# A three-block perceiver on one core: the first rounds re-ordered, the last ones written out by themselves

## The chip, the cores and the metric

The kernel runs on one core of one Trainium2 chip. The metric is the device time of one execution in microseconds (us), and the figure that counts is the median over the runs.

## The reference, cut to what matters

The batch is 32 sequences of 64 rows (x) with a context of 128 rows each; every row has 512 features, all in 32-bit floats.

```python
def reference(x, ctx, ...):
    x = x + xattn(layernorm(x), ctx)   # 16 heads, latent size 32, softmax over 128 keys
    x = x + attn(layernorm(x))         # one head of 128, softmax over 64 keys, then Wo and bo
    x = x + ffn(layernorm(x))
    return x

def ffn(x):
    xh = x @ hadamard
    step = clip(max|xh| per row, 1e-5) / 7
    xq = clip(round(xh / step), -8, 7) * step
    scale = clip(mean|weight| per row of weight, 1e-5)
    wq = where(weight > scale/2, 1, where(weight < -scale/2, -1, 0)) * scale
    return xq @ wq.T
```

## The kernel before

Two sequences make a pair, which fills the 128 partitions; there are 16 pairs (`PAIRS`). Every engine runs the same software pipeline, written as `body(i, ...)` for a round i. A round works on four pairs at once: `front` is pair i+1 (projections of queries and context, and the raw scores of the 16 heads), `cross` is pair i (maxima, 256 exponentials of 128 columns over all pairs, so 16 a round; their transposes; the weighted sum u), `self_` is pair i-1 (the product with Wv, xo; the residual x2; its normalised form x2n; the second attention; x3) and `quant` is pair i-2 (the Hadamard product, the 4-bit quantiser, the product with the ternary weights, the result). Rounds go from -1 to 17. Rounds -1 to 3 and 12 to 17 are unrolled by `pipeline` and `looped`, rounds 4 to 11 run in a hardware loop of two rounds. Stages whose pair does not exist are left out, so that round 15 has no front, round 16 no front and no cross, round 17 only quant.

Nothing plans the order: each engine executes its own list in the order in which `body` writes it, and waits on semaphores: `made[...]` is raised by TensorE (PE) when a PSUM bank is filled, `read[...]` by the engine that has emptied it, `done[...]` by VectorE (DVE), ScalarE (ACT) or GpSimd (POOL). So a wait in one engine's list holds everything written behind it on that engine. PSUM has eight banks: 0 to 3 hold the scores of one pair and then their transposes, B1 to B4 are shared by the other stages in turn.

The parts that matter here, with the line numbers of the profile. On PE: `keep_busy` (L589) issues matmuls on constants that nobody reads; `wide_bias` (L604), `wide_scale` (L610), `hadamard_mean` (L617) and `ternary_transposed` (L627) prepare the weights; `transposed` (L638) turns the exponentials; L648 is xo, L655 turns x3, L691 the Hadamard product, L698 turns x2n, L706 and L709 are `projected`, L729 and L733 queries, keys and values of the second attention, L741 the query projection of two pairs at once in the odd rounds, L786 u, L806 the scores of the next pair, L829 the integer product (L824 its last one in halves), L838 the output projection. On ACT: the exponentials (L320), and all copies out of PSUM under the one line L314. On DVE: `largest` (L450 the maxima of 8 heads, L454 their scaled negatives nmx), `sums` (L459), `ternary` (L429 to L442), the quantiser (L499 to L511), x3 (L580). On POOL: `hadamard_centred` (L274), x2n (L284), x2b (L298), the result (L307).

The weights are prepared within the first rounds. In round 0 DVE runs `ternary` in one piece behind the maxima of pair 0: the sizes of all weight rows (L429), then eight passes that make the ternary matrix, then `const_row`; only behind them come the sums of pair 0 and the maxima of pair 1. PE runs `keep_busy(10, B3)` ahead of the first `transposed` and `keep_busy(4, B3)` behind the last; both `ternary_transposed` stand at the end of round 0. In round 1 PE computes `hadamard_mean` between the projections and the turning of x2n. In rounds 15 to 17 the order is that of every other round, with `keep_busy` in eight places, 29 of its matmuls in all (58 instructions of the trace).

## Time and profile before

| | |
|---|---|
| median of 3 runs | 324.0 us (323.95, 324.0 and 1033.37) |
| profiled execution, its own time | 324.15 us |
| span from first to last instruction in it | 322.4 us |
| busy share of the span | PE 96%, DVE 76%, ACT 65%, POOL 27% |
| granted TensorE clock, mean | 0.999 |

The span is what the trace shows; 1.75 us of the execution's own time lie around it. Busy time of PE counts the constant matmuls of `keep_busy` too. PE's matmuls are pipelined, so that one alone looks longer than its share of a run of them: twenty matmuls of 128 columns take 2.39 us, 0.11 us each. A matmul on 32-bit floats is two instructions in the trace, a transpose of them is one.

### The profile page before, as it was taken

The page shows a single profiled execution, that of the slowest core. Times are in us where ns is not written, and L with a number is a line of the kernel's source. Part 1 is how long each engine was busy: PE and PEld are TensorE (multiplying, and loading weights), DVE is VectorE, ACT ScalarE, POOL GpSimd, SP SyncE. Part 2 cuts the span into 40 slices and gives each one's busy share as a digit, 9 for nine tenths or more (in the row PEclk, how much of TensorE's full clock was granted, in tenths as well). Part 3 has the DMA queues.
Part 4 walks back from the last instruction along what each step waited for, and adds up shares of the span by engine and source line. Part 5 has one row for each costly group of instructions (what it writes and reads, how often), then busy time and mean ns, then how long its engine had stood idle before and what let it go on. Part 6 is the DMA issues. An engine that isn't in the chain of part 4 may idle for free.

```text
span 322.4 us, 8517 instructions
## 1 busy us (share of the span) xinstructions
PE 310.4 (96%) x3172; PEld 219.1 (68%) x3172; DVE 244.9 (76%) x524; ACT 209.5 (65%) x590; POOL 88.4 (27%) x129
## 2 busy tenths in 40 slices
PE   7987999999999999999999999999999999999995
PEld 6875776768576866667576867666675867675754
DVE  1499558887889878887889778987888877986435
ACT  1395867768596777767686777766776869582310
POOL 2000544041223324140323224240414123232320
PEclk9999999999999999999999999999999999999999
DMA  7891402050301403050302302050401010000000
GB/s 205 299 380 63 166 3 98 2 165 32 108 27 38 161 2 130 0 193 2 130 0 89 107 33 98 0 195 0 130 3 68 0 68 2 33 3 33 0 35 33
DMA packets 13481, 25.25 MB, mean 78 GB/s; under 512 B 3216, under 2 KB 3984, under 8 KB 13456
## 3 DMA queue, kind: packets, MB, share of 16 engines
q1 hardware_dynamic: 13456, 24.91, 22.4%
q8 instruction: 16, 0.26, 0.3%
q14 instruction: 9, 0.07, 0.1%
HBM read 20.71 MB, written 4.19 MB: 77 GB/s over the span
## 4 chain that ended last, share of the span: by engine, by line
PE 77%; DVE 10%; ACT 7%; issue 2%; DMA 1%; SPq 0%; POOL 0%; DVEq 0%
PE ps L691 12%; PE ps L729 8%; PE ps L638 7%; PE ps L806 6%; PE ps L786 5%; PE ps L648 4%; PE ps L829 4%; PE ps L838 4%; ACT prob L320 4%; PE ps L733 4%; DVE mx L450 3%; PE ps L709 2%; PE ps L741 2%; PE ps L669 2%; PE ps L812 2%
## 5 line engine op out<-in xcount | busy, mean ns | idle before, releaser
L320 ACT ACTIVATE prob<-ps,nmx,qk_scale 128x128 f32<-128x128 f32 x256 | 96.1, 468 | 40.5 <-DVE nmx L454 40.5
L691 PE MATMUL ps<-had_s,x3t 128*128 128x512 f32 x128 | 59.0, 604 | 1.1 <-ACT x3t L314 0.8
L450 DVE TENSOR_REDUCE mx<-ps 128x8 f32<-128x1024 f32 x32 | 38.9, 1216 | 11.1 <-PE ps L806 11.1
L691 PEld LDWEIGHTS ps<-had_s,x3t 128*128 128x128 f32 x128 | 23.0, 189 | 30.2 <-issue 28.4
L459 DVE TENSOR_REDUCE sum_a<-prob 128x8 f32<-128x1024 f32 x32 | 38.1, 1210 | 2.6 <-ACT prob L320 2.6
L303 POOL TENSOR_TENSOR qk_scale<-aux,power 128x1 f32<-128x1 f32 x16 | 8.8, 548 | 103.9 <-DVE aux L540 103.9
L314 ACT ACTIVATE prob_t<-ps 128x512 f32<-128x512 f32 x64 | 35.2, 622 | 0.6
L638 PE MATMUL ps<-ident,prob 128*128 128x128 f32 x256 | 33.7, 275 | 0.6 <-ACT prob L320 0.6
L729 PE MATMUL ps<-x2t,wqkv_s 128*128 128x128 f32 x256 | 32.7, 281 | 0.6 <-ACT x2t L314 0.2
L307 POOL TENSOR_TENSOR res<-prod,x 128x512 f32<-128x512 f32 x15 | 19.1, 1272 | 47.1 <-DVE prod L573 47.1
L729 PEld LDWEIGHTS ps<-x2t,wqkv_s 128*128 128x128 f32 x256 | 29.8, 191 | 2.6 <-ACT x2t L314 1.8
L638 PEld LDWEIGHTS ps<-ident,prob 128*128 128x128 f32 x256 | 28.5, 141 | 2.4 <-ACT prob L320 1.5
L648 PEld LDWEIGHTS ps<-wv_bd,u_t 128*128 128x128 f32 x128 | 16.7, 191 | 9.1 <-issue 9.1
L281 POOL TENSOR_TENSOR rstd<-aux,power 128x1 f32<-128x1 f32 x16 | 8.8, 548 | 44.6 <-DVE aux L479 44.6
L298 POOL TENSOR_TENSOR x2b<-x,const_row 128x512 f32<-128x512 f32 x16 | 20.3, 1271 | 0.1
L806 PE MATMUL ps<-ckv,q_t 32*64 32x128 f32 x1024 | 19.3, 278 | 0.1
L648 PE MATMUL ps<-wv_bd,u_t 128*128 128x128 f32 x128 | 16.9, 275 | 1.7 <-issue 1.7
L786 PE MATMUL ps<-prob_t,ckv_k 128*32 128x256 f32 x256 | 17.1, 385 | 0.7 <-ACT q_t L314 0.5
L589 PE MATMUL ps<-mean_w 128*128 128x128 f32 x102 | 15.9, 299 | 1.4 <-POOL p L261 1.4
L499 DVE TENSOR_REDUCE amax<-ps 128x1 f32<-128x512 f32 x16 | 11.0, 689 | 8.1 <-PE ps L691 7.9
L806 PEld LDWEIGHTS ps<-ckv,q_t 32*64 32x64 f32 x1024 | 15.5, 130 | 2.4 <-issue 0.7
L589 PEld LDWEIGHTS ps<-mean_w 128*128 128x128 f32 x102 | 14.3, 209 | 4.0 <-issue 2.2
(120 smaller groups left out, 552.7 us busy)
## 6 DMA issues: line engine op xcount, KB each, us to landing
ct<-ctx_cols SPq DMA_DIRECT2D x16, 512.0 KB, 4.6
xt<-x_cols SPq DMA_DIRECT2D x16, 256.0 KB, 2.7
xr<-x_rows SPq DMA_DIRECT2D x16, 256.0 KB, 4.3
y<-res SPq DMA_DIRECT2D x15, 256.0 KB, 2.0
w_rows<-weight SPq DMA_DIRECT2D x1, 1024.0 KB, 8.8
had_s<-hadamard SPq DMA_DIRECT2D x1, 1024.0 KB, 9.0
wqkv_s<-wqkv SPq DMA_DIRECT2D x1, 768.0 KB, 10.6
wqk<-w_qk SPq DMA_DIRECT2D x2, 128.0 KB, 4.5
```

The lines of the kernel that those rows point to most:

```text
L298: nc.gpsimd.tensor_tensor(x2b[:], x2[:], const_row[:], ALU.add).then_inc(done["x2b"], 1)
L314: return nc.scalar.activation(dst, src, ACT.Copy)
L320: last = nc.scalar.activation(prob[:, h, :], ps[:, h // 4, (h % 4) * P:(h % 4) * P + P], ACT.Exp, bias=nmx[:, h:h + 1], scale=qk_scale[:])
L450: V.tensor_reduce(mx[:, h], ps[:, 2 * half:2 * half + 2, :].rearrange("p r (c k) -> p (r c) k", c=EC), AX.X, ALU.max).then_inc(done["mx"], 1)
L459: V.tensor_reduce(sum_a[:, h], prob[:, h, :], AX.X, ALU.add).then_inc(done["sum"], 1)
L589: pe.matmul(ps[:, bank, 0:P], mean_w[:], mean_w[:], start=True, stop=True)
L638: mm = pe.transpose(ps[:, r, c * P:(c + 1) * P], prob[:, 4 * r + c, :], ident[:])
L648: mm = pe.matmul(ps[:, B1, c * P:(c + 1) * P], u_t[:, c, :], wv_bd[:, c, :], start=True, stop=True)
L691: mm = pe.matmul(ps[:, B4, :], x3t[:, c, :], had_s[:, c, :], start=(c == 0), stop=(c == EC - 1))
L729: mm = pe.matmul(ps[:, B1, s * P:(s + 1) * P], wqkv_s[:, c, s * P:(s + 1) * P], x2t[:, c, :], start=(c == 0), stop=(c == EC - 1))
L786: mm = pe.matmul(ps[32 * r:32 * r + 32, B2, :].rearrange("p (c t) -> p c t", c=EC) [:, :, 64 * bb:64 * bb + 64], ckv_k[:, bb, :], prob_t[: ...
L806: mm = pe.matmul(ps[64 * bb:64 * bb + 64, r, c * P:(c + 1) * P], q_t[g, 1 - par, bb, c, :], ckv[g, 1 - par, bb * SKV:(bb + 1) * SKV], star ...
```

## The change

Rounds are re-ordered at both ends; the arithmetic stays, and rounds 3 to 14 are as before. `N` is 15, the last pair. New buffers are added for the last pair's quantiser (`x3t_n`, `aux3_n`, `step_n`, `prod_n` and so on).

At the front. SP issues `had_s`, `w_rows` and the second `load_rows` earlier and `wqkv_s` behind the loads of pair 2. In round 0 PE runs `projected`, the Hadamard mean in two halves, all four `transposed`, `wide_bias` and then the scores of pair 1 ahead of u; DVE takes over three of ACT's copies (q_t, ckv and the first prob_t), and computes only the weight sizes and scales ahead of both maxima of pair 1. The ternary matrix is made in four pieces: three in round 1, the fourth in round 2 between the maximum of the Hadamard product (L499) and the step (L504); its transposes are two halves, one late in round 1, one in round 2 between the values and `transposed(2)`, with ACT's copy of 1024 columns ahead of its copies prob_t 2 and 3. On POOL `hadamard_centred` goes to the start of round 1, behind the first nmx of pair 1. In round 1 PE runs `transposed(2)`, `transposed(3)`, the turning of x2n and the query projection ahead of the second attention's queries.

At the back. From the end of round 14 each engine has a list of its own. The calls of PE and DVE are in the diff; ACT's and POOL's follow the same order of pairs, ACT with all sixteen exponentials of pair 15 together (only the copies of x3t between the sixth and seventh). The maxima of heads 8 to 15 of pair 15 are first in DVE's list; pair 15's xo follows its u directly; the quantiser of pair 14 runs beside the second attention of pair 15. In the text below the written-out part is called the tail. `keep_busy` is called there with 4, 2, 4, 14 and 4. The helpers (`attended`, `head`, `quantized` and so on) issue the same instructions as `body` did, with bank and pair as arguments, and are not shown.

```diff
-        def looped(eng, body):
+        N = PAIRS - 1
+
+        def looped(eng, body, end):
             at = pipeline(body)
             with eng.Fori(*LOOP) as j:
                 body(j * 2, j, 0, True, True, True, True)
                 body(j * 2 + 1, j, 1, True, True, True, True)
-            for i in range(2 * LOOP[1], PAIRS + 2):
+            for i in range(2 * LOOP[1], end):
                 at(i)
...
+            sp.dma_start(had_s[:], hadamard.rearrange("(c p) n -> p c n", p=P)).then_inc(ld_w["had"], 16)
+            sp.dma_start(w_rows[:], weight.rearrange("(c p) n -> p c n", p=P)).then_inc(ld_w["w"], 16)
+            load_rows(1, 1)
             for s in range(3):
                 sp.dma_start(b_qkv[:, s:s + 1], bqkv.rearrange("(s p o) -> s p o", p=P, o=1)[s]).then_inc(ld_w["b"], 16)
             sp.dma_start(bo_row[:], bo.rearrange("(o n) -> o n", o=1).to_broadcast([P, E])).then_inc(ld_w["b"], 16)
-            sp.dma_start(w_rows[:], weight.rearrange("(c p) n -> p c n", p=P)).then_inc(ld_w["w"], 16)
             sp.dma_start(wo_s[:], wo).then_inc(ld_w["wo"], 16)
             sp.wait_ge(zero_wv, 1)
             for r in range(4):
                 sp.dma_start(wv_bd[32 * r:32 * r + 32, :, 32 * r:32 * r + 32],
                              wv_u.rearrange("l (c r d) -> l c r d", c=EC, r=4)[:, :, r, :]).then_inc(ld_w["wv"], 16)
-            load_rows(1, 1)
-            sp.dma_start(had_s[:], hadamard.rearrange("(c p) n -> p c n", p=P)).then_inc(ld_w["had"], 16)
-            sp.dma_start(wqkv_s[:], wqkv.rearrange("(c p) n -> p c n", p=P)).then_inc(ld_w["wqkv"], 16)
             sp.wait_ge(made["lat"], 1)
             load_queries(2, 0)
             load_context(2, 0)
+            sp.dma_start(wqkv_s[:], wqkv.rearrange("(c p) n -> p c n", p=P)).then_inc(ld_w["wqkv"], 16)
...
                 pool.wait_ge(hmean_read, 1)
+                pool.wait_ge(done["nmx"], 3)
                 for c in range(EC):
                     nc.gpsimd.tensor_tensor(had_s[:, c], had_s[:, c], had_mean[:], ALU.subtract).then_inc(had_ready, 1)
...
+                if isinstance(i, int) and i == 1:
+                    hadamard_centred()
...
-                if isinstance(i, int) and i == 1:
-                    hadamard_centred()
...
-            looped(pool, body)
+            looped(pool, body, N)
...
+                if isinstance(i, int) and i == 0:
+                    latents()
...
+                    if not (isinstance(i, int) and i == 0):
+                        pt_copy(0)
                     pt_copy(1)
+                if isinstance(i, int) and i == 1:
+                    x2_turned()
+                    pt_copy(2)
+                    pt_copy(3)
+                    act.wait_ge(made["qt"], 3)
+                    q_copy(0, 0)
...
+                if isinstance(i, int) and i == 2:
+                    ternary_copy(1, 0)
...
+                if isinstance(i, int) and i == 0:
+                    act.wait_ge(hmean_made, 1)
+                    copy(had_mean[:], ps[:, B3, :]).then_inc(hmean_read, 1)
...
-            def ternary():
+            def weight_sizes():
                 dve.wait_ge(ld_w["w"], 16)
-                V.tensor_reduce(w_abs[:], w_rows[:], AX.X, ALU.add, apply_absolute_value=True).then_inc(wabs_done, 1)
-                dve.wait_ge(wabs_done, 1)
+                for c in range(EC):
+                    V.tensor_reduce(w_abs[:, c:c + 1], w_rows[:, c, :], AX.X, ALU.add, apply_absolute_value=True)\
+                        .then_inc(wabs_done, 1)
...
+                if first and i == 0:
+                    dve.wait_ge(made["qt"], 2)
+                    V.tensor_copy(q_t[:, 1], ps[:, B2, :].rearrange("p (c b q) -> p b c q", c=EC, b=2)).then_inc(read["qt"], 1)
+                    dve.wait_ge(made["ckv"], 2)
+                    V.tensor_copy(ckv[:, 1], ps[:, B1, 0:2 * SKV]).then_inc(read["ckv"], 1)
+                    sums(0)
+                    dve.wait_ge(made["pt"], 1)
+                    V.tensor_copy(prob_t[:, 0, :, :], ps[:, 0, :].rearrange("p (c t) -> p c t", c=EC)).then_inc(read["pt"], 1)
                     dve.wait_ge(ld_w["b"], 64)
                     V.tensor_copy(bv_wide[:], b_qkv[:, 2:3].to_broadcast([P, P])).then_inc(bvw_done, 1)
-                    ternary()
-                    dve.wait_ge(cb_made, 1)
-                    V.tensor_tensor(const_row[:], ps[:, B4, :], bo_row[:], ALU.add).then_inc(const_ready, 1)
+                    row_variance()
+                    dve.wait_ge(done["exp"], 2)
+                    row_scale()
+                    sums(1)
+                    weight_sizes()
+                    weight_scales()
+                    dve.wait_ge(made["s"], 2)
+                    largest(1, 0)
+                    largest(1, 1)
+                if first and i == 1:
+                    output_bias()
+                    dve.wait_ge(done["rsum"], 1)
+                    sums(0)
+                    ternary(0)
+                    sums(1)
+                    second_query()
+                    ternary(1)
+                    row_variance()
+                    row_scale()
+                    second_max()
+                    ternary(2)
+                    V.tensor_copy(w_wide[:], w_scale[:].unsqueeze(2).to_broadcast([P, EC, P])).then_inc(wide_done, 1)
...
                         .then_inc(done["amax"], 1)
+                    if first and i == 2:
+                        ternary(3)
...
+            quantized(N - 2, B4, amax, floor3, step_raw, qinv)
+            after(dve, done["sum"], N, 2)
+            after(dve, done["xm"], N - 1)
+            V.reciprocal(rsum[:], sum_a[:].rearrange("p (r c) -> p c r", r=4)).then_inc(done["rsum"], 1)
+            attended(N, 1)
+            second_max(N - 1, B3)
+            second_variance(N)
+            clipped(N - 2, B4)
+            second_sum(N - 1)
+            V.tensor_scalar(qscale[:], step_raw[:], rstd3[:], None, ALU.mult).then_inc(done["qscale"], 1)
+            scaled(N - 2)
+            third_rows(N - 1, B3)
+            third_variance(N - 1, aux3)
+            second_max(N, 0)
+            second_sum(N)
+            third_rows(N, 0)
+            third_variance(N, aux3_n)
+            quantized(N - 1, B4, amax, floor3, step_raw, qinv)
+            clipped(N - 1, B4)
+            after(dve, read["int"], N - 2)
+            V.tensor_scalar(qscale[:], step_raw[:], rstd3[:], None, ALU.mult).then_inc(done["qscale"], 1)
+            quantized(N, 3, amax_n, floor3_n, step_n, qinv_n)
+            V.tensor_scalar(qscale_n[:], step_n[:], rstd3_n[:], None, ALU.mult).then_inc(done["qscale"], 1)
+            clipped(N, 2)
+            scaled(N - 1)
...
                 if cross:
                     if first and i == 0:
-                        keep_busy(10, B3)
+                        keep_busy(4, B4)
+                        after(pe, read["lat"], i + 1)
+                        projected()
+                        hadamard_mean(0, 2)
                     transposed(0)
                     transposed(1)
                 if first and i == 0:
-                    after(pe, read["lat"], i + 1)
-                    projected()
-                    wide_bias()
-                if self_:
-                    if first and i == PAIRS:
-                        keep_busy(2, 0)
+                    hadamard_mean(2, EC)
+                if first and i == 1:
+                    transposed(2)
+                    transposed(3)
+                    x2_turned()
+                    paired_projection()
...
+                if first and i == 2:
+                    pe.wait_ge(read["pt"], i * 4 + 1)
+                    ternary_transposed(1, 0)
...
                 if first and i == 0:
-                    keep_busy(4, B3)
-                if first and i == 1:
...
+                    wide_bias()
...
+                if first and i == 0:
+                    scores()
+                if cross:
+                    weighted_sum()
+                if first and i == 1:
+                    ternary_transposed(0, B4)
+                if self_:
+                    after(pe, done["exp2"], i - 1, 2)
+                    pe.transpose(ps[:, B3, 0:P], p2[:], ident[:]).then_inc(made["p2t"], 1)
+                if front and not (first and i == 0):
+                    scores()
...
-                    if first and i == PAIRS + 1:
-                        keep_busy(2, 0)
...
+                if first and i == 1:
+                    wide_scale()
...
-            looped(pe, body)
+            looped(pe, body, N)
...
+            after(pe, read["ckvk"], N)
+            attended(N - 1, B1)
+            x3_turned(N - 2, B3)
+            after(pe, read["int"], N - 3)
+            head(N - 2, x3t, B4, 0, 2)
+            rows_turned(0)
+            rows_turned(1)
+            head(N - 2, x3t, B4, 2, 3)
+            rows_turned(2)
+            rows_turned(3)
+            head(N - 2, x3t, B4, 3, EC)
+            after(pe, read["lat"], N)
+            x2_turned(N - 1, B2)
+            pe.wait_ge(read["pt"], N * 4 + 4)
+            for bb in range(2):
+                for r in range(4):
+                    mm = pe.matmul(ps[32 * r:32 * r + 32, 0, :].rearrange("p (c t) -> p c t", c=EC)[:, :, 64 * bb:64 * bb + 64],
+                                   ckv_k[:, bb, :], prob_t[:, r, :, 64 * bb:64 * bb + 64], start=True, stop=True)
+            mm.then_inc(made["u"], 1)
+            after(pe, read["x2t"], N - 1)
+            query_key(0, B1)
+            attended(N, 1)
+            query_key(1, B1).then_inc(made["qk"], 1)
+            values(B2)
+            second_scores(N - 1, B3)
+            quantized_turned(N - 2, B4)
+            keep_busy(4, 0)
+            p2_turned(N - 1, B3)
+            after(pe, read["qit"], N - 2)
+            for c in range(EC):
+                mm = pe.matmul(ps[:, B4, :], qi_t[:, c, :], tern_t[:, c, :], start=(c == 0), stop=(c == EC - 1))
+            mm.then_inc(made["int"], 1)
+            second_values(N - 1, B3)
+            x2_turned(N, 2)
+            second_output(N - 1, B3)
+            after(pe, read["x2t"], N)
+            query_key(0, 3)
+            query_key(1, 3).then_inc(made["qk"], 1)
+            x3_turned(N - 1, B3)
+            values(2)
+            second_scores(N, 0)
+            after(pe, read["int"], N - 2)
+            head(N - 1, x3t, B4, 0, 2)
+            p2_turned(N, 0)
+            head(N - 1, x3t, B4, 2, 3)
+            second_values(N, 0)
+            keep_busy(2, B1)
+            second_output(N, 0)
+            head(N - 1, x3t, B4, 3, EC)
+            x3_turned(N, 1)
+            keep_busy(4, B1)
+            head(N, x3t_n, 3, 0, 3)
+            quantized_turned(N - 1, B4)
+            head(N, x3t_n, 3, 3, EC)
+            after(pe, read["qit"], N - 1)
+            for c in range(EC):
+                mm = pe.matmul(ps[:, B4, :], qi_t[:, c, :], tern_t[:, c, :], start=(c == 0), stop=(c == EC - 1))
+            mm.then_inc(made["int"], 1)
+            keep_busy(14, B1)
+            quantized_turned(N, 2)
+            keep_busy(4, B1)
+            after(pe, read["qit"], N)
+            for h in range(2):
+                for c in range(EC):
+                    mm = pe.matmul(ps[:, h, 0:E // 2], qi_t[:, c, :], tern_t[:, c, h * E // 2:(h + 1) * E // 2],
+                                   start=(c == 0), stop=(c == EC - 1))
+                mm.then_inc(half_int, 1)
```

## Rows read from the trace of the kernel before

**Rows 1.** The page: busy time by engine, and the chain that ended last

```profile
PE 310.4 (96%) x3172; PEld 219.1 (68%) x3172; DVE 244.9 (76%) x524; ACT 209.5 (65%) x590; POOL 88.4 (27%) x129
...
PE 77%; DVE 10%; ACT 7%; issue 2%; DMA 1%; SPq 0%; POOL 0%; DVEq 0%
```

**Rows 2.** Busy us (instructions) by stretch: length, PE, PEld, DVE, ACT, POOL; clock, DMA share, GB/s

```profile
28.83:47.63 18.80, 18.40 (x201) 13.26 (x202) 11.10 (x22) 13.57 (x38) 8.43 (x9) 1.00 0.21 72
47.63:64.43 16.80, 16.53 (x174) 11.43 (x173) 14.01 (x31) 12.79 (x38) 3.89 (x6) 1.00 0.13 48
...
277.71:317.61 39.90, 37.42 (x237) 26.47 (x236) 24.69 (x59) 15.13 (x46) 11.28 (x15) 1.00 0.06 21
```

**Rows 3.** The same stretch, instructions of line L589 alone

```profile
277.71:317.61 39.90, 8.09 (x58) 7.42 (x58) 1.00 0.06 21
```

**Rows 4.** Timeline, rounds 0 and 1: start us, length us, engine, line, operation, count

```profile
16.44 2.28 DVE L429 TENSOR_REDUCE w_abs<-w_rows 128x4 f32<-128x2048 f32 x1
...
18.09 2.95 ACT L320 ACTIVATE prob<-ps,nmx,qk_scale 128x128 f32<-128x128 f32 x8
...
24.62 1.21 PE L806 MATMUL ps<-ckv,q_t 32*64 32x128 f32 x64
...
25.16 2.33 DVE L459 TENSOR_REDUCE sum_a<-prob 128x8 f32<-128x1024 f32 x2
...
28.65 1.16 DVE L450 TENSOR_REDUCE mx<-ps 128x8 f32<-128x1024 f32 x1
...
29.91 0.23 DVE L454 TENSOR_SCALAR nmx<-mx,qk_scale 128x8 f32<-128x8 f32 x1
...
31.49 3.70 PE L617 MATMUL ps<-had_s,mean_w 128*128 128x512 f32 x8
...
33.97 0.37 DVE L454 TENSOR_SCALAR nmx<-mx,qk_scale 128x8 f32<-128x8 f32 x1
...
36.15 1.85 ACT L320 ACTIVATE prob<-ps,nmx,qk_scale 128x128 f32<-128x128 f32 x5
...
47.83 0.75 DVE L580 SCALAR_TENSOR_TENSOR x<-ps,rsum,x2b 128x512 f32<-128x512 f32 x1 [0.35 <-PE ps L838]
```

**Rows 5.** Groups by line: count, busy us, mean ns, idle before

```profile
L314 ACT ACTIVATE tern_t<-ps 128x1024 bf16<-128x1024 bf16 x2 | 1.9, 1021 | 1.3 <-PE ps L627 1.3
...
L442 DVE SCALAR_TENSOR_TENSOR tern<-w_rows,w_half,w_neg 128x512 bf16<-128x512 f32 x4 | 3.0, 751 | 0.1
...
L274 POOL TENSOR_TENSOR had_s<-had_s,had_mean 128x512 f32<-128x512 f32 x4 | 5.0, 1272 | 3.0 <-ACT had_mean L314 3.0
```

**Rows 6.** Timeline, round 2

```profile
58.36 1.08 ACT L314 ACTIVATE prob_t<-ps 128x512 f32<-128x512 f32 x2
...
59.77 1.07 PE L786 MATMUL ps<-prob_t,ckv_k 128*32 128x256 f32 x16
```

**Rows 7.** Timeline, the last ten microseconds

```profile
314.05 2.39 PE L589 MATMUL ps<-mean_w 128*128 128x128 f32 x20
...
316.21 0.43 DVE L511 TENSOR_SCALAR qi<-z 128x512 bf16<-128x512 f32 x1
...
317.61 1.05 PE L824 MATMUL ps<-tern_t,qi_t 128*128 128x256 bf16 x8
...
318.43 0.48 DVE L567 SCALAR_TENSOR_TENSOR prod<-ps,qscale,scale_row 128x256 f32<-128x256 f32 x1 [0.75 <-PE ps L824]
```

**Rows 8.** The page, DMA issues: times, KB each, us from issue to landing

```profile
had_s<-hadamard SPq DMA_DIRECT2D x1, 1024.0 KB, 9.0
```

**Rows 9.** Timeline, TensorE, the same eight matmuls twice, and a late start

```profile
8.67 2.08 PE L706 MATMUL ps<-lat,wqk 128*128 128x128 f32 x8
...
18.85 1.06 PE L706 MATMUL ps<-lat,wqk 128*128 128x128 f32 x8
...
28.83 1.13 PE L648 MATMUL ps<-wv_bd,u_t 128*128 128x128 f32 x8 [1.75 <-issue]
```

497 lines of the change are left out of this document (361 added, 136 removed).

## The prediction

> **What bounds the kernel now.** I read the page first. PE is busy 96% of the span and carries 77% of the chain that ended last [rows 1]; so in the middle a round costs what PE issues, and the change leaves rounds 3 to 14 alone. Nothing can be won there. The two ends are different. By stretch, the 39.9 us from the start of round 15 (277.71) to the last integer product (317.61) hold 37.4 us of PE busy time, but DVE is busy 24.7 and ACT only 15.1 [rows 2], and 8.1 us of PE's are the 58 matmul instructions of L589, which compute nothing [rows 3]. At the front the timeline shows serial stretches: pair 1's first nmx comes at 29.91, its second at 33.97, and the last exponentials of pair 1 end at 36.15 + 1.85 = 38.0 [rows 4], while DVE does weight work that is first used in rounds 1 and 2. So I date the new order step by step at both ends, in the trace's own clock, with durations of before.
>
> **The front, round 0.** PE reaches the keep-busy matmuls at 14.8 as before. New order: 4 of them (8 instructions of 0.11 us, the rate of the twenty in [rows 7]) to 15.7; `projected` to 17.2 (the same eight matmuls take 1.06 us, [rows 9], and two wider ones); half the Hadamard mean, 4 of 8 instructions in 3.7 us, less the last one's drain 1.7 [rows 4], to 18.9; transposes 0 and 1 to 19.8; the other half to 21.5; transposes 2 and 3 to 22.4; `wide_bias` to 23.3. ACT still ends pair 0's exponentials at 18.09 + 2.95 = 21.04 [rows 4], as the copy of the latents only changes places, and its copies end at 23.15. So the scores of pair 1 run 23.3 to 24.5; before they began at 24.62 and ended at 25.8 [rows 4].
> DVE: maxima of pair 0 to 16.4, two copies to 17.9, sums 1.2 us each (2.33 for two, [rows 4]), the first prob_t copy after PE's transpose at 19.5, the bias copy, the row variance, second sums: 22.8. Weight sizes: 2.28 us in one piece [rows 4]; in four I take 2.65 (0.14 fixed each, worked out from 1.21 us for 1024 columns and 2.28 for 2048), scales 0.65: 26.1. Pair 1's maxima then: nmx at 27.6 and 29.1. Before: 30.1 and 34.3. The gain so far is 2.5 us on the first half.
>
> **Round 1.** ACT: eight exponentials 2.95, the latents 0.5, eight more: 27.7 to 34.05, against 38.0 before. PE loses the Hadamard mean here (3.7 us, [rows 4]), which had covered this wait; it now stands still about 29.0 to 30.6 and 31.5 to 34.1, 4.2 us in two pieces. So DVE's and ACT's chain is what is late, not PE. From 34.1 PE's list is dense: two transposes 0.9, x2n 0.45, the projection 1.0, queries and keys 1.8, values 0.9, then scores of the second attention, ckv, u, half of the ternary transposes (0.5), p2, the scores of pair 2, o2 and ckv: together 8.4 us by their counts, 9.3 with the waits for the copies of x2t and of the ternary half (1.02 us, [rows 5]). POOL's four centring passes, 1.27 us each [rows 5], run 27.6 to 32.7 ahead of x2n, which is then ready at 34.2, still before PE asks at 35.0: cover, with 0.8 us to spare. DVE does three ternary pieces (0.49 + 0.75 and a gap, 1.3 each; the 0.75 is in [rows 5]) between its duties and is just in time. `wide_scale` and the output projection end at 45.2, so x3 of pair 0 starts at 45.2 instead of 47.83 [rows 4]: 2.6 us gained.
>
> **Round 2 gives some back.** ACT has one more copy of 1.02 us [rows 5] ahead of prob_t 2 and 3, which before started at 58.36 and ended at 59.44; PE started u at 59.77 [rows 6]. Then u can start 1.0 us later less the 0.3 us by which PE was late: 0.75 us. The fourth ternary piece on DVE (1.3 us) stands where DVE waited 0.6 for POOL and later 1.0 for PE, so I cost it nothing; without that cover it would be 0.7. PE's eight transposes (0.5) lie under ACT's copy. Front: 2.6 - 0.75 = 1.85. Bounds: 3.3 if round 2 hides the copy and x3 comes 0.7 sooner, 0.4 if round 2 costs 1.7 and round 1 another 0.5. I take 1.8, as each dated step lies on a row.
>
> **The loads.** `had_s` took 9.0 us from issue to landing [rows 8]. Issued at 5.6 it lands at 14.6 by that row, wanted at 17.2. As a bound: if it landed as late as now (13.25 + 9.0 = 22.3), PE would stand 5.1 us and the whole gain of the front with it. `w_rows` is not wanted before 22.8. wqkv_s moves behind 0.75 MB, 2 us, and has 10 in hand.
>
> **The tail.** PE's real work from 277.71 to the last integer product is a count: three Hadamard products 96 passes of 128 columns, queries, keys and values of two pairs 48, everything else some 111, 255 x 0.111 = 28.3 us. Before, 58 fills add 6.4 and 5.2 us are waits and drains (39.9 in all, [rows 2]). After, 56 fills add 6.2. The waits that remain, from laying the lists of DVE, ACT and POOL beside it: 0.8 for the first x3t copy (as now), 0.4 for the second half of the exponentials, 0.1 for k2, 1.05 for the exponentials of pair 14's second attention (DVE comes to their maximum only after xo, x2 and statistics of pair 15), and 0.05: 2.4. Sum 28.3 + 6.2 + 2.4 = 36.9, so the last product starts 3.0 us earlier. What goes: the three latencies in a row of rounds 15 to 17, because pair 15's x2 is made at 291 in pair 14's shadow and pair 14's quantiser under pair 15's attention. What is late next: DVE's quantiser of pair 15. It needs 2.5 us from the end of its Hadamard product to qi (316.21 + 0.43 = 316.64, less 314.1, where the product had ended and the fill starts, [rows 7]); the list puts the integer product 0.86 and 28 fills, 3.1 us, between, so PE's own list overshoots by 1.3 us and that is in the sum. Behind it: 0.82 from the last product's start to the first half's scaling (317.61 to 318.43, [rows 7]) and 4.0 to the end of the span, as now; DVE's scaling of pair 14 (0.75) ends before, and pair 14's store goes out just ahead of the last two. Bounds of the tail: 4.3 if the overshoot and nothing else goes, 0.5 if each of the some twenty hand-overs is 0.12 us longer than I laid it.
>
> **Sum.** 1.8 + 3.0 = 4.8 us: span 322.4 - 4.8 = 317.6, own time 324.15 - 4.8 = 319.35. The profiled execution is 0.15 above the median of 324.0, so the median comes to 319.2 us, 1.5% less. (A difference of under 2%, 6.5 us, is about what a measurement of this kernel can't tell from none.)
>
> **Rivals.**
> More than that: the copy in round 2 is hidden (0.75) and the tail's waits of 0.4 and 1.05 close up with part of PE's overshoot: 324.0 - 4.8 - 0.75 - 1.2 = 317.2. For it: ACT is the emptiest engine of the tail [rows 2]. Against: the wait of 1.05 is DVE's list order, and nothing moves it.
> The tail doesn't pay: a fixed list waits wherever one engine is late, and x3, x2 and the maxima pass through DVE three times more tightly than before. If the waits take back what they lost, only the front stays: 324.0 - 1.8 = 322.2. For it: 24.7 us of DVE work [rows 2] now has to fit into 37. Against: it has 12 us in hand.
> The clock falls, slower than before. In round 1 PE would be idle 4.2 of 5.1 us, from 29.0 to 34.1. The matmuls of L706 took 2.08 us at 8.67 and 1.06 at 18.85 [rows 9]: the 1.2 and the 2.4 GHz level, and the lower one lasted some ten microseconds from PE's first instruction at 1.4. Against: after the 1.75 us of idleness before 28.83 eight matmuls took 1.13 us [rows 9], the upper level. If the clock falls at 34 and stays low over the 9.7 us of PE work that round 1 still has, that work takes 9.7 more: 319.2 + 9.7 = 328.9. It makes the kernel slower from 4.8 us of PE work at the lower level on. The Trainium skill ("TensorE: Matmul & The Clock Gate", "What's actually happening") says that the gate halves the clock after a stretch without activity and opens it after one of sustained work; by that rule the transposes between the two pauses (0.9 us) decide, and no row of this case has a pause as long as 2.6 us in the middle.
> The load of `had_s` late, as above: 324.0 - 3.0 - 1.8 + 5.1 = 324.3 at most.
>
> **Chances.** Forecast 0.50, its own range 317.5 to 320.6; more than that 0.22; the tail doesn't pay 0.19; the clock 0.06; the load 0.03. Faster by over 2% (under 317.5) are the second case and a little of the first: 0.24; slower by over 2% (above 330.5) a third or so of the clock's, with the low level over round 2 too: 0.03; the rest, 0.73, within 2%. The range goes from 316.5 (rival one with half its own spread) to 322.4 (the tail's rival), and leaves out the clock and the load.
>
> **What would show it.** Right: the scores of pair 1 at 23 to 24.5, their first nmx near 27.6 and second near 29; two pauses of PE before 34; x3 of pair 0 near 45.2; a round 2 of 17.5 instead of 16.8; round 15 beginning near 275.9; the last integer product 36.9 us behind it; fills of L589 still running when the last qi is ready. Wrong: eight matmuls of 128 columns at 2 us anywhere after 30 (the clock), a long wait of PE for a DMA ahead of the Hadamard mean, DVE without idle time in the tail, or PE waiting for qi in place of overshooting.

## The result, and the profile after

The changed kernel takes **318.98 us** (median of 4 executions, 318.38 to 320.26) against 323.98 (median of 4 executions, three of them 323.14 to 324.0, one 1033.37 as above): a ratio of 0.9847, 95% interval 0.9819 to 0.9875, so 5.0 us or 1.5% less. The forecast was 319.2. A second measurement of the same kernel, below, gave 320.35; over all ten executions the median is 319.4.

The page of the changed kernel; one line of DMA issues stands for those that moved:

```profile
span 317.5 us, 8452 instructions
PE 305.5 (96%) x3131; PEld 215.1 (68%) x3146; DVE 247.0 (78%) x530; ACT 208.1 (66%) x587; POOL 89.4 (28%) x129
PEclk9999999999999999999999999999999999999998
PE 77%; DVE 11%; ACT 7%; issue 2%; DMA 2%; SPq 0%; DVEq 0%
had_s<-hadamard SPq DMA_DIRECT2D x1, 1024.0 KB, 7.8
```

The shares are those of [rows 1]: PE at 96%, 77% of the chain. PE is busy 4.9 us less, and the span is 4.9 us shorter (322.4 to 317.5), so over the whole span PE stands still as long as before: 12.0 us. The shares don't say which waits went and which came. By stretch they are these: from the first scores to xo of pair 0 PE stood 2.9 us and now stands 0.5; in round 1 it was 0.4 and is 3.0, as the Hadamard mean went to round 0; from round 15 to the last integer product 2.5 and now 0.8. A part of the busy time that went is fills: the first 28 us hold 24 constant instructions instead of 44, 5.4 us instead of 7.8. Those weren't what held PE. In the kernel before it waited for ACT right behind them:

```profile
17.92 1.09 PE L638 MATMUL ps<-ident,prob 128*128 128x128 f32 x8 [0.63 <-ACT prob L320]
...
23.62 1.07 PE L786 MATMUL ps<-prob_t,ckv_k 128*32 128x256 f32 x16 [0.54 <-ACT q_t L314]
```

(No run takes the fills alone out of the kernel before.) The timeline of PE after the change, in rounds 0 and 1 (start us, length us, engine, line, operation, count, idle time before and its releaser):

```profile
12.56 1.20 PE L1103 MATMUL ps<-ckv,q_t 32*64 32x128 f32 x64
...
23.72 1.20 PE L1103 MATMUL ps<-ckv,q_t 32*64 32x128 f32 x64
...
30.31 1.09 PE L934 MATMUL ps<-ident,prob 128*128 128x128 f32 x8 [0.80 <-ACT prob L368]
33.48 1.09 PE L934 MATMUL ps<-ident,prob 128*128 128x128 f32 x8 [2.08 <-ACT prob L368]
```

The first line is pair 0's scores, the second pair 1's: they begin at 23.72, in [rows 4] at 24.62, although this execution started its first scores 0.42 later than the one before did (12.14). The two transposes L934 show the two pauses of PE that were forecast. DVE and ACT in the same rounds, and DVE's first line of round 2:

```profile
22.93 2.46 DVE L567 TENSOR_REDUCE w_abs<-w_rows 128x1 f32<-128x512 f32 x4
...
27.09 0.23 DVE L600 TENSOR_SCALAR nmx<-mx,qk_scale 128x8 f32<-128x8 f32 x1
...
28.56 0.23 DVE L600 TENSOR_SCALAR nmx<-mx,qk_scale 128x8 f32<-128x8 f32 x1
...
27.36 2.90 ACT L368 ACTIVATE prob<-ps,nmx,qk_scale 128x128 f32<-128x128 f32 x8 [0.67 <-DVE nmx L600]
...
30.48 2.95 ACT L368 ACTIVATE prob<-ps,nmx,qk_scale 128x128 f32<-128x128 f32 x8
...
45.16 0.75 DVE L754 SCALAR_TENSOR_TENSOR x<-ps,rsum,x2b 128x512 f32<-128x512 f32 x1 [0.66 <-PE ps L1135]
```

Pair 1's nmx, at 29.91 and 33.97 in [rows 4], now starts at 27.09 and 28.56; its exponentials end at 33.4, not 38.0; x3 of pair 0 follows at 45.16, 2.67 us sooner. Two stretches, round 2 and from round 15 to the last integer product, with the columns of [rows 2]:

```profile
44.96:62.48 17.52, 16.99 (x181) 11.88 (x181) 16.17 (x33) 13.64 (x39) 3.94 (x6) 1.00 0.14 47
275.83:312.51 36.68, 35.91 (x233) 25.57 (x234) 24.03 (x59) 15.24 (x46) 10.01 (x14) 1.00 0.04 15
```

In [rows 2] they were 16.80 and 39.90 us. So round 2 is 0.72 longer and the tail 3.22 shorter. The timeline of round 2, PE, ACT, DVE and POOL:

```profile
57.82 1.07 PE L1083 MATMUL ps<-prob_t,ckv_k 128*32 128x256 f32 x16
...
55.76 1.02 ACT L362 ACTIVATE tern_t<-ps 128x1024 bf16<-128x1024 bf16 x1
56.68 1.08 ACT L362 ACTIVATE prob_t<-ps 128x512 f32<-128x512 f32 x2
...
52.41 1.87 DVE L587 SCALAR_TENSOR_TENSOR tern<-w_rows,w_half,w_neg 128x512 bf16<-128x512 f32 x1
...
52.47 1.26 POOL L314 TENSOR_TENSOR x2b<-x,const_row 128x512 f32<-128x512 f32 x1
```

Counted from the round's start, prob_t comes 11.72 us in, where [rows 6] has 10.73, and u on PE 12.86 in, where they have 12.14. The end of the tail:

```profile
308.22 3.29 PE L886 MATMUL ps<-mean_w 128*128 128x128 f32 x28
311.34 0.39 PE L1141 MATMUL ps<-ident_b,qi 128*128 128x128 bf16 x4
...
312.51 1.04 PE L1273 MATMUL ps<-tern_t,qi_t 128*128 128x256 bf16 x8
...
309.52 0.43 DVE L802 TENSOR_SCALAR qi<-z 128x512 bf16<-128x512 f32 x1
...
313.77 0.71 DVE L880 TENSOR_TENSOR res<-prod_n,x 128x256 f32<-128x256 f32 x1
...
312.93 1.26 POOL L347 TENSOR_TENSOR res<-prod,x 128x512 f32<-128x512 f32 x1 [8.61 <-DVE prod L825]
```

qi is ready at 309.95, but PE turns it at 311.34, behind 28 matmuls that compute nothing. From the last integer product to the end of the span it is now 4.99 us (317.5 - 312.51), where it was 4.79 (322.4 - 317.61).

### The profile page after: what moved, and what is told of

Its sections match the earlier page's. It is cut to its first block, busy times and chain, and to the rows that moved or that the text cites. A ratio compares the mean times of both kernels' runs of the same rounds, so it can differ in the third digit from the quotient of the medians.

```text
span 317.5 us, 8452 instructions
## 1 busy us (share of the span) xinstructions
PE 305.5 (96%) x3131; PEld 215.1 (68%) x3146; DVE 247.0 (78%) x530; ACT 208.1 (66%) x587; POOL 89.4 (28%) x129
## 3 DMA queue, kind: packets, MB, share of 16 engines
q1 hardware_dynamic: 13456, 24.91, 23.3%
## 4 chain that ended last, share of the span: by engine, by line
PE 77%; DVE 11%; ACT 7%; issue 2%; DMA 2%; SPq 0%; DVEq 0%
PE ps L983 10%; PE ps L1037 9%; PE ps L934 6%; PE ps L1103 5%; ACT prob L368 4%; PE ps L1083 4%; PE ps L1041 4%; PE ps L1158 3%; PE ps L1135 3%; PE ps L944 3%; PE ps L1129 3%; PE ps L1010 2%; DVE mx L596 2%; PE ps L994 2%; PE ps L886 2%
## 5 line engine op out<-in xcount | busy, mean ns | idle before, releaser
L368 ACT ACTIVATE prob<-ps,nmx,qk_scale 128x128 f32<-128x128 f32 x240 | 89.9, 469 | 34.1 <-DVE nmx L600 34.0
L983 PE MATMUL ps<-had_s,x3t 128*128 128x512 f32 x104 | 48.0, 604 | 0.3 <-ACT x3t L362 0.3
L605 DVE TENSOR_REDUCE sum_a<-prob 128x8 f32<-128x1024 f32 x30 | 35.8, 1209 | 0.5 <-ACT prob L368 0.5
L983 PEld LDWEIGHTS ps<-had_s,x3t 128*128 128x128 f32 x104 | 18.7, 189 | 24.7 <-issue 22.8
L934 PE MATMUL ps<-ident,prob 128*128 128x128 f32 x240 | 31.6, 275 | 2.9 <-ACT prob L368 2.9
L934 PEld LDWEIGHTS ps<-ident,prob 128*128 128x128 f32 x240 | 26.8, 141 | 5.4 <-ACT prob L368 4.3
L1037 PE MATMUL ps<-x2t,wqkv_s 128*128 128x128 f32 x224 | 28.6, 281 | 0.4
L1037 PEld LDWEIGHTS ps<-x2t,wqkv_s 128*128 128x128 f32 x224 | 26.1, 191 | 2.1 <-ACT x2t L362 1.4
L321 POOL TENSOR_TENSOR res<-prod,x 128x512 f32<-128x512 f32 x13 | 16.6, 1274 | 32.7 <-DVE prod L747 32.7
L314 POOL TENSOR_TENSOR x2b<-x,const_row 128x512 f32<-128x512 f32 x14 | 18.2, 1301 | 0.0
L1041 PE MATMUL ps<-wqkv_s,x2t 128*128 128x128 f32 x112 | 14.8, 275 | 0.0
L1135 PE MATMUL ps<-wo_s,o2t 128*128 128x512 f32 x28 | 14.3, 592 | 0.0
L886 PE MATMUL ps<-mean_w 128*128 128x128 f32 x80 | 12.6, 305 | 1.4 <-POOL p L274 1.4
```

The lines of the kernel that those rows point to most:

```text
L368: last = nc.scalar.activation(prob[:, h, :], ps[:, h // 4, (h % 4) * P:(h % 4) * P + P], ACT.Exp, bias=nmx[:, h:h + 1], scale=qk_scale[:])
L605: V.tensor_reduce(sum_a[:, h], prob[:, h, :], AX.X, ALU.add).then_inc(done["sum"], 1)
L934: mm = pe.transpose(ps[:, r, c * P:(c + 1) * P], prob[:, 4 * r + c, :], ident[:])
L983: mm = pe.matmul(ps[:, B4, :], x3t[:, c, :], had_s[:, c, :], start=(c == 0), stop=(c == EC - 1))
L1037: mm = pe.matmul(ps[:, B1, s * P:(s + 1) * P], wqkv_s[:, c, s * P:(s + 1) * P], x2t[:, c, :], start=(c == 0), stop=(c == EC - 1))
L1041: mm = pe.matmul(ps[:, B2, 0:P], x2t[:, c, :], wqkv_s[:, c, 2 * P:3 * P], start=(c == 0), stop=(c == EC - 1))
```

## The experiments

Three questions: is the gain the sum of the two ends, what does each named step cost, and why do equal kernels differ by more than 1 us? The kernel before had medians of 323.82, 324.73 and 324.0 us in the three sets of executions that follow.

**Each half alone.** `front_only`: the new `body` and loads, with the old last rounds:

```diff
-            second_norm(N - 1)
...
-            result(N - 1)
+            looped(pool, body, PAIRS + 2)
```

(the same on the other engines).

> The new rounds -1 to 2, with rounds 15 to 17 as before. Theory (the two ends add up): the front is worth 1.9 us, so 322.1 us, and x3 of pair 0 starts near 45.2 in the trace. Rival (the tail hides part of what the front gains, or needs it): under 1 us, above 323.0.

Measured: 322.51 (ratio 0.9941, 0.9912 to 0.9971, 10 executions). `tail_only` is the reverse, the old loads and `body` with the new last rounds:

```diff
-                if isinstance(i, int) and i == 0:
-                    latents()
...
+                if front:
```

> Rounds -1 to 14 as before, the last rounds written out. Theory: the last integer product starts 36.7 us after round 15 begins, in place of 39.9, and the end of the span keeps its 4.8 to 5.0 us behind it: 3.0 us less, 321.0 us. Rival (the front carries most of the gain): above 322.5.

Measured: 321.25 (ratio 0.9922, 0.9894 to 0.995). Its last integer product starts 36.70 us behind round 15's xo, as in the whole change (36.68). The gains are 1.3 and 2.6 us, together 3.9; with the intervals that is no contradiction to 5.0, but the front is at the low end. The executions of `front_only` fall into two groups: the four with a mean granted clock of 0.997 or more took 321.49 to 321.87, the six at 0.995 or less 322.5 to 324.49. So the first group has a gain of 2.0 us, where the forecast for the front was 1.8, and something takes it from the others.

**The clock in round 1.** The profiled execution of `front_only` had the clock fall there, and so had `fill_8`, `no_fill`, `scaled_first` and `tern_behind` below, though none of them changes round 1. So the changed kernel was run again, unchanged:

> The changed kernel once more, for its spread. Theory: the clock falls in round 1 in a part of its executions and this, beside the start, is what spreads them: median 319.2 us (318.8 to 319.6), and the executions with a mean clock of 0.995 or less take 1 to 2 us more than those at 0.997 and more. Rival, the spread is the first loads' alone: no relation between the mean clock and the time.

Measured: 320.35 (318.86 to 321.8, 6 executions; ratio 0.9872, 0.984 to 0.9904), 0.75 above the range expected here. One execution, the fastest, had a clock of 1.0; the others had 0.988 to 0.995 and took 319.32 to 321.8, so 0.5 to 2.9 us more, where 1 to 2 were expected. The mean clock is a rough sign only. It also counts a fall behind PE's last product: the first profile has 0.997 with 1.00 in all of round 1, and `best_a` below 0.996. And the start moves as much as the clock: in `scaled_first` below, executions at 0.992 and 0.995 took 318.76 to 318.94, and one at 1.0 took 318.83. The profiled one, PE in round 1, then the columns of [rows 2] in steps of 2 us:

```profile
31.38 1.09 PE L934 MATMUL ps<-ident,prob 128*128 128x128 f32 x8 [0.81 <-ACT prob L368]
34.56 1.93 PE L934 MATMUL ps<-ident,prob 128*128 128x128 f32 x8 [2.08 <-ACT prob L368]
```

```profile
34.00:36.00 2.00, 1.44 (x7) 1.45 (x8) 1.96 (x3) 1.48 (x4) 1.80 (x3) 0.66 0.79 254
36.00:38.00 2.00, 2.00 (x13) 1.67 (x13) 1.27 (x2) 0.62 (x2) 1.26 (x1) 0.50 0.08 31
38.00:40.00 2.00, 2.00 (x25) 1.88 (x22) 1.12 (x3) 1.44 (x3) 0.00 (x0) 0.99 0.04 8
```

The pauses are those of the first profile, 0.81 and 2.08 us against 0.80 and 2.08. Yet there the transposes behind them took 1.09 us and here 1.93, the 1.2 GHz level (0.50 over the next two microseconds). By the granted clock that is 2 x 0.34 + 2 x 0.50 = 1.7 us, a part of it while PE still stood idle. The Trainium skill ("TensorE: Matmul & The Clock Gate", "What's actually happening") names two levels, says that recent activity chooses between them, and that the monitor does not start its count with the kernel, so that equal kernels differ. These two profiles agree. Whether the pauses are the cause was tested by filling them (`pause_fill`):

```diff
                 if cross:
+                    if first and i == 1:
+                        pe.wait_ge(hmean_read, 1)
+                        keep_busy(6, B3)
...
                 if first and i == 1:
+                    keep_busy(9, B3)
                     transposed(2)
```

> The changed kernel with constant matmuls in the two pauses of TensorE in round 1: 6 calls ahead of transposed(0), 9 ahead of transposed(2), 1.3 and 2.0 us, in bank B3, less than the pauses of 1.3 and 2.1 us. Theory (the pauses let the clock fall in some executions, which costs them 1 to 2 us): all executions keep a mean granted clock of 0.997 or more, none is above 320 us, and the median falls by 0.5 to 1.0, to 318.2 us. Rival (the spread of the changed kernel comes from the loads at the start alone): the spread and the median stay as they are, or the fills run over into the transposes and cost 0.3 us.

Measured: 318.61 (ratio 0.9825, 0.9795 to 0.9854), all six executions at 0.998 or more, 317.99 to 319.6. PE in round 1:

```profile
28.35 1.60 PE L886 MATMUL ps<-mean_w 128*128 128x128 f32 x12
29.79 1.04 PE L934 MATMUL ps<-ident,prob 128*128 128x128 f32 x8
30.66 2.17 PE L886 MATMUL ps<-mean_w 128*128 128x128 f32 x18
32.67 1.04 PE L934 MATMUL ps<-ident,prob 128*128 128x128 f32 x8
```

From first scores to x3 of pair 0 it is 32.61 us, as in the changed kernel's first profile (32.60); the kernel before needed 35.69. The profile of the fall has 34.48, but 0.47 of that lies ahead of round 1, since its first scores took 1.67 us instead of 1.20. So the cost is better counted from the second transposes to x3: 11.68 us in the first profile, 11.40 here, and 12.99 to 13.24 in the seven profiles of this round 1 whose clock fell. A fall costs 1.3 to 1.6 us, of a front that wins 3.1 up to x3. In three of the seven (`fill_8`, `no_fill`, `tern_behind`) the eight transposes behind the second pause still took 1.09 us, and the level fell behind them.

Why do the fills delay nothing, though they put the second transposes 0.3 us later (21.21 us behind the first scores, not 20.92)? What PE wants next is POOL's x2n. In the first profile:

```profile
33.58 0.95 POOL L300 TENSOR_SCALAR x2n<-x,aux,rstd 128x512 f32<-128x512 f32 x1 [0.20 <-POOL rstd L297]
34.59 0.66 PE L1002 MATMUL ps<-ident,x2n 128*128 128x128 f32 x4
```

(In `pause_fill` they start at 32.51 and 33.55.) It is ready 21.97 and 21.99 us behind the first scores, and PE takes it 0.06 and 0.10 later. So the chain through DVE and POOL (the centring passes stand ahead of x2n) ends together with the one through ACT's exponentials, and earlier exponentials alone would win little; no run moves the centring passes. The medians of `pause_fill` and of the changed kernel have overlapping intervals; what is shown is that the clock stays up in every execution, and it does so in round 1 of the two other profiles with these fills (`best_a`, `best_b`) too. So the open pauses are the cause of the falls; why a given execution is spared is not shown.

**The order of the loads** (`loads_old`): all loads issued in the order of before, all else changed. The lines of `had_s`:

```diff
-            sp.dma_start(had_s[:], hadamard.rearrange("(c p) n -> p c n", p=P)).then_inc(ld_w["had"], 16)
...
             load_rows(1, 1)
+            sp.dma_start(had_s[:], hadamard.rearrange("(c p) n -> p c n", p=P)).then_inc(ld_w["had"], 16)
```

> The changed kernel with the loads in the order of before. The PE has to stand at the Hadamard mean of round 0 until had_s lands, at 22.3 in the trace of before, where it wants it at 17.5: the first half of the mean comes 4.8 us later; ct of pair 0 lands 0.46 us earlier. Theory (the order of the loads is what lets the front work): 4 us slower than the changed kernel, 323.0 us. Rival (it is only an order): 319 us or 0.4 less.

Measured: 326.74 (325.82 to 327.86; ratio 1.0084, 1.006 to 1.0108), slower than before the change. PE's timeline, and two stretches:

```profile
21.69 3.29 PE L913 MATMUL ps<-had_s,mean_w 128*128 128x512 f32 x4 [3.55 <-DMA had_s<-hadamard]
24.78 1.46 PE L934 MATMUL ps<-ident,prob 128*128 128x128 f32 x8
26.07 1.88 PE L913 MATMUL ps<-had_s,mean_w 128*128 128x512 f32 x4
```

```profile
22.00:24.00 2.00, 2.00 (x4) 0.73 (x3) 0.00 (x0) 0.00 (x0) 0.00 (x0) 0.55 1.06 406
40.00:42.00 2.00, 2.00 (x11) 1.81 (x9) 2.00 (x2) 0.31 (x1) 2.00 (x2) 0.50 0.23 90
```

The wait is there, 3.55 us, and PE's clock falls behind it: the same four matmuls take 3.29 us and then 1.88. It falls again in round 1. First scores to x3 takes 39.38 us here, 6.8 more than 32.6. The wait and the 1.4 us of those four are 5.0 of them, the transposes behind (1.46 for 1.04) 0.4, and the fall in round 1 costs 1.3 (12.99 - 11.68). The direction was right, but the cost was more than the 4 us that I had put: 6.4 to 7.8 by the medians (against 320.35 and 318.98), since the long wait of PE is paid for a second time by the lower level behind it.

**The copy in round 2** (`tern_behind`):

```diff
-                if isinstance(i, int) and i == 2:
-                    ternary_copy(1, 0)
                 if cross and not (isinstance(i, int) and i == 1):
...
                     pt_copy(3)
+                if isinstance(i, int) and i == 2:
+                    ternary_copy(1, 0)
```

> The changed kernel with ACT's copy of the second ternary half in round 2 moved behind the copies of prob_t 2 and 3. Theory (round 2 gives back 0.7 us because u waits for prob_t 3, which stands behind this copy): u starts 0.7 us earlier, but the exponentials of the second attention and ckv are held by the copy, so the scores of pair 3 gain 0.1 to 0.4 at most: round 2 lasts 17.2 us instead of 17.52. Rival (TensorE's own list is the bound of round 2): 17.5 us still.

Measured: 319.77 (ratio 0.9872, 0.9828 to 0.9917), round 2 17.84 us in place of 17.52; the expectation failed. PE, then ACT:

```profile
57.77 1.07 PE L1083 MATMUL ps<-prob_t,ckv_k 128*32 128x256 f32 x16
59.10 0.33 PE L1115 MATMUL ps<-ident,p 128*128 128x128 f32 x1 [0.27 <-ACT p L452]
...
56.35 1.08 ACT L362 ACTIVATE prob_t<-ps 128x512 f32<-128x512 f32 x2 [0.53 <-PE ps L934]
57.32 1.03 ACT L362 ACTIVATE tern_t<-ps 128x1024 bf16<-128x1024 bf16 x1
58.23 0.30 ACT L452 ACTIVATE p<-ps,nmx 64x64 f32<-64x64 f32 x1
```

The theory had put u 0.7 us earlier and the round at 17.2. u comes 12.66 us into the round, only 0.2 sooner than 12.86: ACT is free, and now waits 0.53 for PE, whose eight ternary transposes are what is late. And the copy, put behind, holds the second attention's exponentials, so that PE's next step waits. The 0.72 us has two covers on top of each other: PE's 0.5 lay under ACT's 1.0, and taking the one away shows the other.

**The fills of the tail.** `fill_8` issues 16 instead of 28 matmuls ahead of the last qi:

```diff
-            keep_busy(14, B1)
+            keep_busy(8, B1)
```

> The changed kernel with 8 instead of 14 constant matmuls ahead of the last turning of qi. Theory (PE overshoots): in the changed kernel qi of pair 15 is ready at 309.95 and PE turns it at 311.34, behind its own fills; 12 instructions fewer end them at 310.0, so the turning comes 1.3 us earlier and the time falls to 317.7 us. Rival (the fills keep the clock up or qi is bound elsewhere): same time within 0.3 us, with the matmuls behind it at the lower level.

Measured: 319.49 (318.0 to 321.15, 4 executions; ratio 0.9871, 0.9823 to 0.9919). In its profile the tail is 35.37 us, 1.31 less, which is the length of the 12 instructions taken out: qi is ready at 309.99 and PE turns it at 310.05. The median doesn't show it (317.7 was expected), and the clock fell in round 1 of the profile. `no_fill` takes all five calls out of the last rounds:

```diff
-            keep_busy(4, 0)
...
-            keep_busy(14, B1)
...
-            keep_busy(4, B1)
```

> The changed kernel without any constant matmul in the written-out last rounds (28 calls fewer). The overshoot of 1.3 us and some fills of 0.4 us that stand ahead of ready work go. Theory (the last fills hold the clock): TensorE then is idle for 2.7 us ahead of the last turning of qi and for 0.9 behind it, the clock falls, and the last products run at the lower level: saving of 1.7 less 1 to 2, so 318.6 us or no change. Rival (the fills do nothing): 317.3 us with the upper level to the end.

Measured: 318.26 (317.0 to 319.77; ratio 0.9814, 0.9779 to 0.9849). PE and DVE at its end, then a stretch:

```profile
310.08 0.40 PE L1141 MATMUL ps<-ident_b,qi 128*128 128x128 bf16 x4 [1.62 <-DVE qi L802]
311.00 1.05 PE L1268 MATMUL ps<-tern_t,qi_t 128*128 128x256 bf16 x8 [0.52 <-DVE qi_t L807]
...
312.26 0.96 DVE L880 TENSOR_TENSOR res<-prod_n,x 128x256 f32<-128x256 f32 x1
```

```profile
310.00:312.00 2.00, 1.40 (x12) 0.93 (x12) 1.49 (x5) 0.00 (x0) 0.32 (x1) 1.00 0.00 0
```

The tail is 34.94 us, 1.74 less. PE now waits for DVE's quantiser (1.62 and 0.52), and the clock is still 1.00. I had expected it to fall, so that theory failed for this execution. Of the fills' 6.2 us only 1.74 had stood on the path, and 0.2 of that goes again behind the last integer product, where the span now needs 5.2 us (316.2 - 311.00), not 4.99.

**The port between DVE and POOL.** In [rows 7] the last results come from DVE alone; after the change the first half takes 0.71, without fills 0.96, beside POOL's L347. `scaled_first` lets POOL start earlier:

```diff
-            clipped(N, 2)
             scaled(N - 1)
+            clipped(N, 2)
```

> The changed kernel with DVE's scaling of pair 14 moved ahead of its clipping of pair 15, into the 1.7 us in which DVE waits there. Then GpSimd's result of pair 14 runs 310.9 to 312.2 instead of 312.9 to 314.2, clear of DVE's first half result, which in the changed kernel took 0.71 us beside it against 0.42 us for the second half. Theory (the two engines' additions, both from two SBUF operands, exclude each other): the first half takes 0.42 us and the end comes 0.3 us sooner. Rival (the 0.71 has another cause): the half still takes 0.7 us and nothing changes.

Measured: 318.81 (318.17 to 320.76; ratio 0.9832, 0.9798 to 0.9866). DVE, then POOL:

```profile
313.72 0.43 DVE L880 TENSOR_TENSOR res<-prod_n,x 128x256 f32<-128x256 f32 x1
...
310.76 1.27 POOL L347 TENSOR_TENSOR res<-prod,x 128x512 f32<-128x512 f32 x1 [6.49 <-DVE prod L825]
```

POOL is through at 312.03, DVE's half takes 0.43, and the end of the span comes 4.63 us behind the last integer product, not 4.99. Where they meet, DVE's end is tied to POOL's: POOL 312.93 + 1.26 = 314.19 and DVE 313.77 + 0.71 = 314.48, 0.29 later; in `no_fill` POOL ends at 312.94 (311.68 + 1.26) and DVE at 313.22, 0.28 later. So DVE doesn't run slowly beside POOL, it stands until POOL is done. The median is not told apart from the changed kernel's; the 0.36 us rest on the profile. The Trainium skill ("SBUF — State Buffer", "Who interferes with whom") says this: a DVE instruction with two SBUF inputs and a GpSimd one that reads SBUF exclude each other, and the second waits for the whole of the first. The numbers agree.

**Together.** `best_a` is `pause_fill` and `no_fill` in one, `best_b` has `scaled_first` as well (the diffs are those above).

> The changed kernel with keep-busy matmuls in the two pauses of round 1 and without any in the last rounds. Theory, both effects stand at different ends and add: clock at 1.00 in round 1, third output of pair 0 32.6 us after the first scores, last integer product 34.9 us after pair 15's output projection starts; median 316.9 us (316.4 to 317.4). Rival, they do not add, because with the upper clock over the whole span the last rounds without filling matmuls lose the clock or the waits take the gain: 318.0 us or more.

Measured: **316.52** (315.93 to 317.53, 5 executions; ratio 0.9771, 0.9746 to 0.9796). First scores to x3 32.61 us, tail 34.94. Measured beside it, the changed kernel had a ratio of 0.9872 (0.984 to 0.9904), so this one beats both kernels, and its median is 0.4 below the forecast of 316.9. (Its mean clocks, 0.993 to 0.996, say nothing against it: in the profile the clock is 1.00 until 310 and falls behind PE's last product.)

> As best_a, with GpSimd scaling pair 15's third output before it clips pair 14's. Theory of the port: the first half of the last result takes DVE 0.43 us in place of 0.96, the span behind the last integer product is 0.3 to 0.5 us shorter; median 316.5 us (316.0 to 317.1). Rival, clipping pair 14 later delays its store and the last stores with it: no shorter than best_a.

Measured: 317.11 (316.16 to 317.58, 5 executions; ratio 0.9777, 0.9752 to 0.9803), just above the range expected and not told apart from `best_a`. DVE's half is 0.42 us, as expected; PE lost more than that. PE, then a stretch:

```profile
308.15 0.40 PE L1145 MATMUL ps<-ident_b,qi 128*128 128x128 bf16 x4 [1.62 <-DVE qi L802]
309.26 1.89 PE L1272 MATMUL ps<-tern_t,qi_t 128*128 128x256 bf16 x8 [0.71 <-DVE qi_t L807]
```

```profile
308.00:310.00 2.00, 1.14 (x8) 0.79 (x9) 1.20 (x4) 0.00 (x0) 1.05 (x1) 0.71 0.00 0
```

Here the clock does fall behind the waits that the missing fills leave, and the last product takes 1.89 us, not 1.05. In `best_a` the first wait was the same (1.61) and the product took 1.05. But the second wait differs, 0.71 for 0.52, and that is the edit's doing: without fills DVE no longer waits 1.7 us for PE there, so the scaling of pair 14 (308.13, 0.74) now stands in front of the clipping of pair 15, which starts 0.64 us behind PE's turning of qi and not 0.44. What was free in `scaled_first` costs 0.2 us here. Whether the longer second wait or chance made the clock fall, one profile of each can't say. As far as they show, the fills at the end guard 0.84 us and cost 1.5, which is no good bargain here.

## Why the prediction was right, by its steps

The time (319.2 for 318.98, or 319.4 over ten) came out, and so did both halves in the profile (1.88 and 3.0 us for 1.8 and 3.0), by the steps that the forecast names; the medians of the halves run alone give 1.3 and 2.6. A few terms inside did not come out, and for two of them the agreement is luck.

| Step | forecast | measured |
|---|---|---|
| scores of pair 1, first and second nmx ready | 23.3, 27.6, 29.1 | 23.72, 27.3, 28.8 |
| PE's pauses in round 1 | 1.6 and 2.6 us | 0.80 and 2.08 |
| x3 of pair 0 | 45.2 | 45.16 |
| round 2 | +0.75 | +0.72 |
| tail to the last integer product | 36.9 | 36.68 |
| overshoot of the fills | 1.3 | 1.31 (`fill_8`) |
| span behind the last integer product | as before | +0.20 |
| whole span | 317.6 | 317.5 |

**Front.** x3 at 45.16 is right by two deviations that cancel, which is luck. The exponentials end at 33.4, not 34.05, although PE's first scores began 0.42 later than before: the four weight sizes took 2.46 and not 2.65, and PE's scores, DVE's chain and the sixteen exponentials together were 1.0 shorter than I laid them. Against that, PE's list from the second transposes to x3 took 11.7 us (33.48 to 45.16) where I had 11.1 (34.1 to 45.2). Of these 0.6, 0.2 are x2n: I gave POOL 0.8 us to spare, and PE waited for it, as its centring passes and x2n took 5.41 and 0.95, in place of 5.1 and the 0.76 of before. The rest is in the list behind it (10.57 from x2n to x3, where I had 10.2). The later start came with the context of pair 0, which landed later; over the profiles of new and old orders of loads that start lies between 10.07 and 13.14 us, so the new order is not shown to be its cause. Counted from the first scores, the front wins 3.1 us up to x3; less 0.42 and 0.72 that is 1.95, and at the start of round 15 1.88 (277.71 - 275.83), for the forecast 1.8.

**Round 2.** The right sum for the right reason, ACT's copy ahead of prob_t; `tern_behind` shows that PE's transposes lay under it, as the step said. The fourth ternary piece was costed at nothing and took 1.87 instead of 0.75 us behind POOL's L314 (it ended at 54.28, 0.55 behind POOL's), but DVE had that room: u still waited for ACT's copies.

**Loads.** `had_s` landed in 7.8 us; PE did not wait. The rival's price for a late load, 5.1 us, was too low: `loads_old` waited only 3.55 but was 6.4 to 7.8 above the changed kernel, the clock being part of it, where I had let the late load cost its wait alone.

**Tail.** It wins 3.22 us, less 0.20 behind the last product, 3.0 as forecast (with the front's 1.88 the span's 4.9). 36.68 for 36.9: with the counted 28.3 of work and 6.2 of fills as they stood in the forecast, 2.2 are left for waits and drains, where I had 2.4. The next in line was DVE's quantiser, as said: without fills PE waits for it. The claim that what follows the last integer product stays as it was failed by 0.2: POOL's last result and DVE's now meet at the port.

**The clock.** This rival had the right place and the wrong size and chance. I made it an exception worth 9.7 us with a chance of 0.06. In fact the clock fell in seven of the eight profiles that have the new round 1 with its pauses open, one of the two of the changed kernel itself among them, and cost 1.3 to 1.6 us, because the full level was back by 38 (0.99) and not only after the rest of the round. My own sign of being wrong, eight matmuls of 128 columns at 2 us after 30, came in that profile (1.93). So the fall could not turn the sign of the change, but it is in the time: three of the ten executions of the changed kernel have a mean clock of 0.988 or 0.989, lower than a fall at the end alone gives in any profile here (0.991 in `best_b`); for the three at 0.993 to 0.995 the mean doesn't tell, and of them only the profiled one is seen to fall in round 1. The forecast's own range (317.5 to 320.6) took the second measurement's 320.35 in without my having put this in; that is luck too. The front's 1.8 us is the gain of an execution whose clock stays up.

**The other rivals.** "The tail doesn't pay" is refuted by `tail_only`. The 317.2 of "more than that" was not reached by closing waits; `best_a` passed it by removing fills at one end and adding them at the other.

What stays open: what decides whether the clock falls behind a given pair of pauses. The two profiles of the same kernel have the same pauses, and differ ahead of them in PE's start: first scores at 12.56 and 13.14 us, of 1.20 and 1.67 us. Open too is what spreads the first scores' start over 3 us. And for the first microseconds the granted clock of the profile can't be used: it is 1.00 from 8 to 10 us, where the matmuls L991 take 2.08 us that take 1.06 at 16.21.

## What to carry to other kernels

Split a change at its two ends and run each end alone; where a part shows two groups of times, sort them by granted clock before explaining the median. When a re-ordering leaves PE with two pauses close together, price the fall of the clock as a chance in each execution (here 1.3 to 1.6 us), and fill the pauses only as long as the engine awaited is surely later; a fill beyond that is on the path itself. A cost hidden under another one is not free: removing the upper one alone brings little. And try a re-ordering again when the wait that it used has been closed by another edit: in `best_b` the scaling held up the step that it had been clear of in `scaled_first`.
